# Who adds the biases in the last four pairs, and when the last batch's heads are masked

## The reference, cut to what matters

```python
q = elu(x @ Wq + bq) + 1;  k = elu(x @ Wk + bk) + 1;  v = x @ Wv + bv
k = k / sqrt(sum(k * k over a head) + EPS)
attn = (q k^T) v                      # no softmax: so q (k^T v), one 16x16 block per head
y = x + attn @ Wo + bo
a = layernorm(y) * gamma + beta
x = layernorm(x + a)
h = silu(fp4(x) @ fp4(w_gate).T) * (fp4(x) @ fp4(w_up).T)
x = layernorm(x + fp4(h) @ fp4(w_down).T)
```

## Time and profile before

| | us |
|---|---|
| median of 3 runs | 718.66 (717.65 to 720.54) |
| the profiled execution: its time | 717.77 |
| its span | 716.0 |
| PE busy in the span | 690.5 |
| Pool busy | 615.6 |
| DVE busy | 589.8 |
| ACT busy | 484.9 |

### The profile page before, as it was taken

The page is one execution under the profiler, slowest core; times in us unless marked ns, Lnnn a source line. Parts: engine busy times, 40 slices in busy tenths (PEclk is TensorE's granted clock), DMA queues, the critical chain, the costliest instruction groups (busy, mean ns, idle before and its releaser), DMA issues.

```text
span 716.0 us, 13705 instructions
## 1 busy us (share of the span) xinstructions
PE 690.5 (96%) x4114; PEld 615.5 (86%) x4114; DVE 589.8 (82%) x1436; ACT 484.9 (68%) x943; POOL 615.6 (86%) x955
## 2 busy tenths in 40 slices
PE   7999999999976999999999999999999999999995
PEld 6888888888865789999999999899999999999995
DVE  6788778876756789989988989989899889898874
ACT  5666676665645767677677677677776776777664
POOL 3989888988997799889889889898898898899767
PEclk9999999999997999999999999999999999999999
DMA  9443343343222001111112111112111121100001
GB/s 280 165 133 133 133 136 133 126 152 135 103 90 89 30 31 49 71 45 60 45 45 74 46 52 53 45 47 73 45 60 46 44 70 50 48 28 16 16 31 44
DMA packets 22269, 55.01 MB, mean 77 GB/s; under 512 B 2546, under 2 KB 5556, under 8 KB 22196
## 3 DMA queue, kind: packets, MB, share of 16 engines
q1 hardware_dynamic: 21776, 54.01, 22.1%
q10 hardware_dynamic: 420, 0.13, 0.2%
HBM read 28.90 MB, written 25.17 MB: 76 GB/s over the span
## 4 chain that ended last, share of the span: by engine, by line
PE 88%; POOL 5%; issue 3%; DVE 2%; DMA 1%; ACT 1%; SPq 0%; POOLq 0%; DVEq 0%
PE banks L366 22%; PE banks L368 21%; PE banks L367 21%; PE banks L499 8%; PE banks L472 7%; PE banks L402 3%; PE banks L377 2%; POOL arena L1022 1%; PE banks L513 1%; PE banks L512 1%; PE banks L429 1%; PE banks L390 1%; DMA arena<-in_L_attn_x_dram 1%; POOL lnbuf L1073 1%; PE banks L437 1%
## 5 line engine op out<-in xcount | busy, mean ns | idle before, releaser
L366 PE MATMUL banks<-wgu_hi,actT_lo 128*128 128x512 f32 (+1 forms) x384 | 150.6, 392 | 1.5 <-DVE actT_lo L883 1.5
L367 PE MATMUL banks<-wgu_lo,actT_hi 128*128 128x512 f32 (+1 forms) x384 | 144.2, 376 | 0.0
L368 PE MATMUL banks<-wgu_hi,actT_hi 128*128 128x512 f32 (+1 forms) x384 | 143.6, 374 | 0.0
L668 ACT ACTIVATE arena<-banks 128x512 f32<-128x512 f32 x64 | 38.4, 600 | 118.0 <-PE banks L368 117.9
L1088 POOL TENSOR_TENSOR arena<-arena 128x960 f32<-128x960 f16 (+2 forms) x68 | 115.1, 1693 | 0.0
L1064 POOL TENSOR_TENSOR arena<-arena 128x704 f32<-128x704 f32 x64 | 89.1, 1393 | 20.8 <-DVE arena L870 18.8
L366 PE MATMUL banks<-wd_hi,actT_lo 128*128 128x256 f32 x320 | 100.1, 313 | 0.0
L883 DVE TENSOR_TENSOR actT_lo<-banks,actT_hi 128x512 fp32r<-128x512 f32 (+1 forms) x132 | 85.6, 674 | 16.3 <-ACT actT_hi L654 15.6
L368 PE MATMUL banks<-wd_hi,actT_hi 128*128 128x256 f32 x320 | 90.2, 282 | 0.0
L367 PE MATMUL banks<-wd_lo,actT_hi 128*128 128x256 f32 x320 | 90.2, 282 | 0.0
L366 PEld LDWEIGHTS banks<-wgu_hi,actT_lo 128*128 128x128 f32 x384 | 72.9, 190 | 10.7 <-DVE actT_lo L883 2.1
(11 more groups left out here) (125 smaller groups left out, 1954.1 us busy)
## 6 DMA issues: line engine op xcount, KB each, us to landing
xs<-x_plus_scratch SPq DMA_DIRECT2D x32, 512.0 KB, 3.2
x_plus_scratch<-xs SPq DMA_DIRECT2D x24, 512.0 KB, 2.9
arena<-in_L_attn_x_dram SPq DMA_DIRECT2D x32, 256.0 KB, 3.7
out_dram<-arena SPq DMA_DIRECT2D x32, 256.0 KB, 2.1
x_plus_scratch<-arena SPq DMA_DIRECT2D x8, 512.0 KB, 2.9
resid<-in_L_ffn_w_down_dram SPq DMA_DIRECT2D x1, 704.0 KB, 7.6
resid<-in_L_ffn_w_gate_dram SPq DMA_DIRECT2D x1, 640.0 KB, 8.3
resid<-in_L_ffn_w_up_dram SPq DMA_DIRECT2D x1, 640.0 KB, 9.1
```

The lines of the kernel that those rows point to most:

```text
L366: nc.tensor.matmul(dst, sl, mh, start=(k == 0), stop=False, skip_group_check=shared)
L367: nc.tensor.matmul(dst, sh, ml, start=False, stop=False, skip_group_check=shared)
L368: last = nc.tensor.matmul(dst, sh, mh, start=False, stop=(ended and k == n - 1), skip_group_check=shared)
```

## The change

DVE runs `x_biases(p)` for p = 28 to 31, at the end of its turn behind `k_sums(p)`; Pool runs them for p up to 27. The waits ahead of them are the same and go with them. Pool's `over_scales` of the first two tiles write where x lay, and now also wait for the sums of the pairs up to 28 and up to 30 (the semaphore `xb_s`). DVE's `mask_heads(7)` moves from the start of turn 34 to turn 33, behind the query features of pair 31. PE, ACT and SP are left as they are.

```diff
+        DVE_BIASES = NP - 4
+
+        def x_biases_free(eng, p):
+
+            eng.wait_ge(x_in[p % PPB], 16 * (p // PPB + 1))
+            if p < MERGE:
+                after(eng, xs_out[p % 2], 16 * (p // 2))
+            else:
+                after(eng, xs_late_out, 16 * (p - MERGE))
...
+            def x_biases(p):
+                if p == DVE_BIASES:
+                    dve.wait_ge(xb_in, 2 * 16)
+                x_biases_free(dve, p)
+                r = p % PPB
+                for kind, row in enumerate((bo_b, beta_b)):
+                    nc.vector.tensor_tensor(xs_late[:, :, kind, :], xin[:, 2 * r:2 * r + 2, :],
+                                            row[:, :].unsqueeze(1).broadcast_to([P, 2, D]), ALU.add).then_inc(xb_s, 1)
...
-                if p >= 6 and (p - 6) % PPB == 0 and (p - 6) // PPB < B:
+                if p >= 6 and (p - 6) % PPB == 0 and (p - 6) // PPB < B - 1:
                     mask_heads((p - 6) // PPB)
                 if pair(p - 2):
                     q_features(p - 2)
+                if p == NP + 1:
+                    mask_heads(B - 1)
...
                 if pair(p):
                     k_sums(p)
+                if pair(p) and p >= DVE_BIASES:
+                    x_biases(p)
...
-                if pair(p):
+                if pair(p) and p < DVE_BIASES:
                     x_biases(p)
...
                 if n < 2:
                     pool.wait_ge(xT_ps, NP - 3 + 2 * n)
+                    pool.wait_ge(xb_s, 2 * (NP - 3 + 2 * n))
```

More of the change, by code:

```diff
@@ L1013, in x_biases @@
             def x_biases(p):
+                x_biases_free(pool, p)
                 r = p % PPB
[L1015 to L1019, removed]
                 to = xs[:, p % 2, :, :, :] if p < MERGE else xs_late
```

## The result

The changed kernel takes 711.35 us (median of 4 runs, 710.39 to 712.29) against 719.6 us of the kernel before on the same chip (4 runs, 717.65 to 720.71). The ratio is 0.9894, with a 95% interval of 0.9874 to 0.9915: 7.6 us less, of 8.4 forecast. Against the median of the three runs before the forecast was 710.3 us, with a range from 706.8 to 715.0. The profiled execution took 711.88 us, its span is 710.1.

The account below looks back on a forecast made before the run. PE bounds 258 to 698 us; only its waits before about 250 count, chained to Pool from 187 to 212. 4.8 (3.9 + 0.9) + 3.6 = 8.4 us less: 709.4 profiled, 710.3 against the median, range 706.8 to 715.0.

Parts of the forecast that it names:

- The loop: From turn 30 a chain through all engines is last; the merge's first dequantise ends 3.9 us earlier, bounds 3.5 and 4.6.
- The cover: DVE's waits of 1.6 to 2.0 us before L736 and L770 hide its adds, 1.3 us a turn, at no cost.
- The two engines in each other's way: Each DVE add costs a busy Pool 0.5 to 0.7 us; two beside the Newton steps take 1.1 us.
- L866: DVE's instruction behind the dequantise in turn 31, slow beside Pool's first add: gives back 0.9 us.
- The mask: Turn 34: PE's 1.96 us wait for the last batch's mask and half clock behind it go, 3.6 us; bounds 2.0, 3.7.
- The rival that the clock takes back what the mask gives: Another wait is as late as Pool's, or the clock undoes the mask's gain: 0 to 3 us, 717 us; chance 0.07.
- The clock: Half clock for 4.2 us behind PE's wait for L906 stays; bounds 2.0 us gained, 2 us lost.

Follow-up runs that it names:

- the adds alone: Changed kernel with the last batch's mask put back to turn 34, adds of the last four pairs still on DVE: ratio 0.9933 to the kernel before.
- adds of one column: Changed kernel with each of DVE's eight adds covering 1 column of a row of 256: ratio 0.9863 to the kernel before.
- the adds ahead: Changed kernel with DVE's adds in front of its key features, not behind the key sums: ratio 0.9946 to the kernel before.
- the kernel before with PE kept busy: Kernel before, with 48 transposes of the identity added in PE's wait of 6.05 us in turn 32: ratio 0.9974.

## Why the prediction was right, point by point

- **The loop.** Forecast 3.9 us forward for the dequantise of turn 31. It ended at 212.29 - 186.58 = 25.7 us from the first mark before and ends at 210.00 - 188.06 = 21.9 after: 3.8. That Pool's adds were in the loop is shown by the adds alone (4.4 us at the product), and that the loop then runs through all engines by Pool's own waits for ACT. Part of the nearness is luck. With adds of one column, where the engines hardly meet, the dequantise ends at 208.93 - 187.56 = 21.4 us: the loop gave 4.3 us, not the 4.6 forecast, and the meetings took 0.6 of it, not 1.1. By these two forecasts the sum was 3.5; the 3.9 was chosen between bounds.
- **The cover.** DVE's adds were to cost nothing by themselves in its waits of 1.6 to 2.0 us. Shown from three sides: with one column only 0.87 us is won, all of it by Pool's standing beside them; twice the work costs 2.66, and the same work ahead of the key features costs 4.1. What I overlooked is turn 30, where DVE waited only 1.04 us ahead of L770 (at 197.02) before the change. The adds of turn 29 use up that wait, and the query features come 0.05 us later against the first mark than with adds of one column.
- **The two engines in each other's way.** Forecast 0.5 to 0.7 us of Pool's time for each add, about 1.1 us in the loop. Measured: 2.4 us over eight adds in Pool's rows, 0.3 each (0.67, 0.64, 0.75 and three times 0.55 against 0.19 to 0.26), and no more than 0.87 us on the path. The size was too high because the first adds of turns 30 and 31 run while Pool waits for ACT's seeds anyway. One reading behind it was wrong: L822 ran from 10.37 to 11.64 us, beside Pool's first add (9.81 to 11.60) and not its second, so that at the start both engines waited in turn. In the run with the adds ahead an add of DVE took up to 1.21 us and an affine of Pool 1.18, so there both wait. The Trainium skill has it so (SBUF — State Buffer, section "Who interferes with whom"): the one that begins later stands still. Pool's affine agrees (it starts at 186.82, behind DVE's add at 186.21), and so do all but one of the six rows of the changed kernel: L1074 is recorded from 196.20, 0.02 us ahead of the add, and yet it is the longer one. In the changed kernel no add waits, all eight lie between 0.682 and 0.687 us. Four of them start while Pool waits, and three within 0.1 us of the start of one of its short instructions; whether that is why none waits, no run shows by itself.
- **L866.** Forecast 0.9 us back; it took 1.17 and takes 0.24. Against it `cut` (0.58 us there before, 0.88 after) takes longer beside Pool's scaling of the keys in turn 32, which I had not counted. So the product came 3.8 + 0.9 - 0.3 = 4.4 us earlier, not 4.8.
- **The mask.** Forecast 3.6; alone it is 3.42, beside the adds 2.65 (30.23 against 27.58 in the rest). The rival that the clock takes back what the mask gives has a part in both: the low clock behind the product cost 0.4 us more than before in the first, 1.3 us more than with the adds alone in the second. DVE waits 0.84 us for PE's last keys and values in turn 33 and has 2.25 us left before it is needed.
- **The clock.** I left 4.2 us at half clock in the sum, with bounds of 2 us to either side. After, it was 6.03 us, about 1 us more lost; with the 0.4 us that the product lacks this is somewhat more than the 1.05 us between 7.35 and 8.4. The runs show the same spread: the clock granted over a whole execution was 0.993 to 0.997 in the four of the changed kernel, and the one at 0.997 took 710.39 us, those at 0.993 711.88 and 712.29.

What I had wrong in reasoning is small in this sum, but not elsewhere: I took the low clock behind the mask as bound to its wait of 1.96 us. The run of the kernel before with PE kept busy has the same wait and no low clock.

## What to carry to other kernels

Work moved to another engine costs what its place in that engine's order makes of it: the same eight adds cost at most 0.9 us behind the key sums and took back nearly all of the gain in front of the key features. Before moving work off an engine that never pauses, follow the semaphores to see what is late next: the loop through all engines gave 3.8 us where Pool was freed of 7.6. Where an engine's wait can't be shortened, look at what follows it: 36 idle transposes were worth up to 2.8 us, two thirds of what moving the adds brought, and the changed kernel with them is the fastest with DVE's order untouched, 708.67 us at a ratio of 0.9855.

## What the runs showed of the hardware

- Behind a PE wait of about 4.7 us the clock was at its lower level for 6.03 us in one profile and at 0.73 on average for the same length in another. Behind the wait of 3.14 to 3.17 us in turn 31, in three profiles of programs that agree up to there, it fell in two and stayed up in one. So code that is the same can differ by more than 1 us in such a place, and a single profile must be read around it.
- Transposes of the identity kept the clock up in the three runs that had them: 36 took 4.09 us, 0.11 each, and the granted clock behind them was 1.00, where it was 0.50 in the changed kernel without them.
- DVE's and Pool's instructions with two operands in SBUF hold each other up in both directions, but a short one pays most: Pool's instructions of 3 columns went from 0.19 to 0.67 us beside DVE's adds, while an add of DVE that began beside an idle Pool took 0.68 us every time. DVE's instructions with one operand are held up too: L866 took 1.17 us beside Pool's add and 0.24 without it, and `cut` of 256 columns took 0.88 beside the scaling of the keys, 0.22 in turn 33 of the changed kernel.
